# The additions to x and the moments of finished tiles, moved from the stage after an LSTM recurrence into the gaps of the recurrence itself

## What is computed

```python
def step(carry, x_t):
    h0, c0, h1, c1, a = carry
    xin = jnp.concatenate([x_t, a], axis=-1)
    h0, c0 = _lstm_cell(xin, h0, c0, Wi0, Wh0, bi0, bh0)
    h1, c1 = _lstm_cell(h0, h1, c1, Wi1, Wh1, bi1, bh1)
    q = h1 @ Wq.T
    attn = softmax(einsum('bh,bsh->bs', q, context))
    mixed = einsum('bs,bsh->bh', attn, context)
    a2 = jnp.tanh(jnp.concatenate([mixed, h1], axis=-1) @ Wo.T + bo)
    return ((h0, c0, h1, c1, a2), a2)

x = x + scan(step, layernorm(x))      # 1024 steps in time, batch of 4
x = x + ffn(layernorm(x))             # its input is quantized with max|layernorm(x)| over the whole tensor
...
```

## Time and profile before

| | |
|---|---|
| Time of the runs, median of 3 | 8434.98 us (8434.35 to 8435.3) |
| The profiled execution's own time | 8436.1 us |
| Its span, from first to last instruction | 8434.3 us |
| PE busy | 6828.4 us (81%) |
| PEld busy | 5803.5 us (69%) |
| DVE busy | 4235.9 us (50%) |
| ACT busy | 3225.4 us (38%) |
| POOL busy | 279.8 us (3%) |
| DMA | 62186 packets, 95.43 MB |
| Mean granted TensorE clock | 0.977 of 2.4 GHz |

### The profile page before, as it was taken

The page is one execution under the profiler, slowest core; times in us unless marked ns, Lnnn a source line. Parts: engine busy times, 40 slices in busy tenths (PEclk is TensorE's granted clock), DMA queues, the critical chain, the costliest instruction groups (busy, mean ns, idle before and its releaser), DMA issues. The chain is left out here.

```text
span 8434.3 us, 813385 instructions
## 1 busy us (share of the span) xinstructions
PE 6828.4 (81%) x380504; PEld 5803.5 (69%) x380505; DVE 4235.9 (50%) x21151; ACT 3225.4 (38%) x15030; POOL 279.8 (3%) x289
## 2 busy tenths in 40 slices
PE   6888888888888888888888888888888888776687
PEld 5777777777777777777777777777777777553454
DVE  5555555554554455455555455545545555565712
ACT  3333333333333333333333333333333333332322
POOL 0000000000000000000000000000000000012501
PEclk8999999999999999999999999999999999888798
DMA  2000000000000000000000000000000000000333
GB/s 85 5 0 0 0 0 0 0 0 0 0 0 0 0 0 0 0 0 0 0 0 0 0 0 0 0 0 0 0 0 0 0 0 0 0 6 18 111 116 112
DMA packets 62186, 95.43 MB, mean 11 GB/s; under 512 B 13633, under 2 KB 50497, under 8 KB 60993
## 3 DMA queue, kind: packets, MB, share of 16 engines
q1 hardware_dynamic: 59072, 86.54, 3.0%
q0 software_dynamic: 3072, 8.39, 0.3%
HBM read 74.99 MB, written 19.92 MB: 11 GB/s over the span
## 5 line engine op out<-in xcount | busy, mean ns | idle before, releaser
L304 PE MATMUL scan_sums<-rec_wh,scan_hT 128*4 128x64 f32 x131008 | 2392.1, 219 | 4.2 <-issue 4.1
L425 DVE STREAM_TRANSPOSE scan_sums<-scan_sums 128x64 f32<-128x64 f32 x6144 | 1546.0, 266 | 1137.6 <-PE scan_sums L304 1137.3
L304 PEld LDWEIGHTS scan_sums<-rec_wh,scan_hT 128*4 128x4 f32 x131008 | 1989.5, 89 | 4.9 <-issue 4.9
L304 PE MATMUL scan_sums<-rec_wa,scan_aT 128*4 128x64 f32 (+1 forms) x65536 | 1104.3, 219 | 382.0 <-ACT scan_aT L385 382.0
L304 PEld LDWEIGHTS scan_sums<-rec_wa,scan_aT 128*4 128x4 f32 (+1 forms) x65536 | 915.4, 88 | 570.9 <-ACT scan_aT L385 570.9
L304 PE MATMUL scan_sums<-rec_wx,scan_xT 128*4 128x64 f32 (+1 forms) x65536 | 1292.1, 219 | 7.7 <-issue 6.8
L304 PE MATMUL scan_sums<-rec_wi,scan_hT 128*4 128x64 f32 (+1 forms) x65536 | 1102.5, 219 | 168.8 <-DVE scan_hT L475 165.2
L304 PEld LDWEIGHTS scan_sums<-rec_wi,scan_hT 128*4 128x4 f32 (+1 forms) x65536 | 913.6, 88 | 357.6 <-DVE scan_hT L475 353.9
L304 PEld LDWEIGHTS scan_sums<-rec_wx,scan_xT 128*4 128x4 f32 (+1 forms) x65536 | 1024.2, 89 | 8.4 <-issue 7.4
L365 ACT ACTIVATE scan_sums<-rec_bias 128x192 f32<-128x192 f32 x2050 | 687.2, 335 | 475.1 <-DVE scan_hT L475 469.5
L370 ACT ACTIVATE scan_tanh_f<-scan_sums 128x8 f32<-128x8 f32 x2048 | 364.1, 178 | 1187.9 <-DVE scan_sums L425 1187.9
(11 more groups left out here) (247 smaller groups left out, 5750.5 us busy)
## 6 DMA issues: line engine op xcount, KB each, us to landing
experts_bias<-in_b SPq DMA_DIRECT2D x40, 640.0 KB, 3.8
moe_w<-in_w SPq DMA_DIRECT2D x16, 1024.0 KB, 12.3
slots_x<-route_zero SPq DMA_DIRECT2D x40, 128.0 KB, 1.7
experts_x<-slots_x SPq DMA_DIRECT2D x40, 128.0 KB, 2.1
slots_y<-experts_y SPq DMA_DIRECT2D x40, 128.0 KB, 1.7
w_xres<-in_x_steps SPq DMA_DIRECT2D x8, 512.0 KB, 11.3
w_xres<-in_x SPq DMA_DIRECT2D x4, 1024.0 KB, 11.7
out<-w_xres SPq DMA_DIRECT2D x8, 512.0 KB, 3.0
```

What stands on the lines that cost most here:

```text
L304: last = nc.tensor.matmul(sums[layer][BANK[g]][32 * j:32 * j + ROWS[g], 0:64], state[:, k, FIRST[g]:FIRST[g] + ROWS[g]], weight[:, k, j, 6 ...
L425: nc.vector.transpose(turned[l][g], sums[l][g][:, 0:64]).then_inc(gates_turned[l][g], 1)
```

## The change

It adds four programs to the recurrence, each working on group g - 1 (the 128 steps that are finished) while the steps of group g run, for g from 1 to 7:

1. GpSimd (L297 to L302) waits until `a_hist` holds the group and until the transposes of the group before are done, and copies the eight pieces (b, k) of 128x128 into `part`.
2. VectorE, in gaps 0 and 1 of the group's steps 0 to 3, transposes a piece in blocks of 32x32 into `stage` (`turn_part`, L496). The blocks are then right within, but not in the right places.
3. SP (L314 to L323) waits for the eight transposes, writes them with 32 transfers, each of 32 partitions x 4 x 32 values, into `a_rows` in DRAM, where the blocks land in order, waits for all, and reads the four tiles back into `mid` with one transfer.
4. VectorE adds the four tiles to x in gaps 0 and 1 of steps 7 and 8 (`fold`, L501), forms the statistics in those of steps 9 and 10 (`spread`, L505 and L506) and 11 and 12 (`gather_moments`, L510 and L511), and keeps the moments in step 13 (`keep_moments`, L515).

VectorE's loop over the steps becomes two: steps 28 to 127 as before, and then a loop over g in which 14 steps are written out and an inner loop runs the other 114. Nothing in TensorE's and ScalarE's recurrence changes.

The stage after the recurrence keeps the additions and moments of the last group's four tiles. TensorE turns them straight out of `a_hist` (L624), before the weights. ScalarE takes the square roots of 28 tiles in one instruction and later of 4 (`deviations`, L641), and it, not VectorE, normalizes all 32 tiles (`normalize`, L645), with the weight copies (L637) between them. VectorE forms the factors (L685, L687) and the largest values (L693). GpSimd's copies are gone from the stage.

```diff
 def scan(nc, ins, xT_all, a_hist, xres, ffn, w_out_scratch, a_rows, w):
...
         with nc.Block() as block:
+            @block.gpsimd
+            def _(pool):
+                nc.gpsimd.sem_inc(staged, 2 * B)
+                with pool.Fori(1, NB) as g:
+                    for b in range(B):
+                        for k in range(2):
+                            pool.wait_ge(a_kept, g * P)
+                            pool.wait_ge(staged, 2 * B * g)
+                            nc.gpsimd.tensor_copy(part[:, b, k, :], a_hist[:, bass.ds(g * P - P, P), k, b]).then_inc(part_done, 1)
+
             @block.sync
             def _(sp):
...
                 sp.wait_ge(ffn["w_out_kept"], 16)
+                for g in range(1, NB):
+                    sp.wait_ge(staged, 2 * B * g + 2 * B)
+                    for b in range(B):
+                        rows = a_rows[b, bass.ds(g * P - P, P), :].rearrange("(q r) (j k u) -> j r k q u", q=4, j=4, k=2)
+                        for j in range(4):
+                            for k in range(2):
+                                sp.dma_start(rows[j][:, k], stage[32 * j:32 * j + 32, b, k, :].rearrange("p (q u) -> p q u", q=4)).then_inc(rows_out, 16)
+                    sp.wait_ge(rows_out, ROWS_OUT * g + ROWS_OUT)
+                    sp.wait_ge(folded, B * g)
+                    sp.dma_start(mid[:], a_rows[:, bass.ds(g * P - P, P), :].rearrange("b p d -> p b d")).then_inc(mid_in, 16)
...
+                def turn_part(g, b, k):
+                    dve.wait_ge(part_done, 2 * B * g)
+                    dve.wait_ge(rows_out, ROWS_OUT * g)
+                    nc.vector.transpose(stage[:, b, k, :], part[:, b, k, :]).then_inc(staged, 1)
+
+                def fold(g, b):
+                    x = tile_of(xres, g - 1, b)
+                    dve.wait_ge(mid_in, 16 * g)
+                    nc.vector.tensor_tensor(x, mid[:, b, :], x, ALU.add).then_inc(folded, 1)
+
+                def spread(g, b):
+                    dve.wait_ge(folded, B * g + B)
+                    nc.vector.memset(held[:, 0:1], 0.0)
+                    nc.vector.bn_stats(stats[:, b, :], tile_of(xres, g - 1, b)).then_inc(spread_done, 1)
...
+                def late(g, at):
+                    def between(gap):
+                        if gap == 2:
+                            return
+                        if at < 4:
+                            turn_part(g, at, gap)
+                        elif 7 <= at < 9:
+                            fold(g, 2 * (at - 7) + gap)
+                        elif 9 <= at < 11:
+                            spread(g, 2 * (at - 9) + gap)
+                        elif 11 <= at < 13:
+                            gather_moments(g, 2 * (at - 11) + gap)
+                        elif at == 13 and gap == 0:
+                            keep_moments(g)
+                    return between
...
-                with dve.Fori((PLAIN + 3 * FC + 1) // U, T // U) as i:
+                with dve.Fori((PLAIN + 3 * FC + 1) // U, P // U) as i:
                     t = i * U
                     for s in range(U):
                         step(t, s)
+                dve.wait_ge(ffn["x_in"], 16 * (B + 1))
+                LATE = 14
+                with dve.Fori(1, NB) as g:
+                    for at in range(LATE):
+                        step(g * P, at, late(g, at))
+                    with dve.Fori(LATE // U, P // U) as i:
+                        t = g * P + i * U
+                        for s in range(U):
+                            step(t, s)
...
 def add_attention_and_normalize(nc, raw, a_hist, xres, xn, norm_max, w):
...
+                for b in range(B):
+                    for k in range(2):
+                        last = nc.tensor.transpose(turned[b][:, P * k:P * k + P], a_hist[:, P * LAST:P * NB, k, b], w["ident"][:])
+                    last.then_inc(turned_done, 1)
...
+                act.wait_ge(eps_done, 1)
+                deviations(0)
+                for f in range(2):
+                    keep_weight(f)
+                act.wait_ge(shift_done, 1)
+                for n in range(B * LAST):
+                    normalize(n)
+                    if n == 2 * B:
+                        act.wait_ge(moments_done, B)
+                        deviations(1)
+                    if n % B == B - 1 and 2 + n // B < FC:
+                        keep_weight(2 + n // B)
+                act.wait_ge(shift_done, 2)
+                for n in range(B * LAST, NT):
+                    normalize(n)
...
```

More of the change, by code:

```diff
@@ L284, in scan @@
         seeded = [m.sem(f"seeded{l}") for l in range(2)]
-        with nc.Block() as block:
+        part = m.sbuf("part", [P, B, 2, P])
+        stage = m.sbuf("stage", [P, B, 2, P])
+        mid = m.sbuf("mid", [P, B, D])
+        stats, moments = m.sbuf("stats", [P, B, 6]), m.sbuf("moments", [P, B, 2])
+        held = m.sbuf("held", [P, 2])
+        part_done, staged, rows_out, mid_in, folded, spread_done, moments_done, moments_kept = (m.sem(n) for n in (
+            "part_done", "staged", "rows_out", "mid_in", "folded", "spread_done", "moments_done", "moments_kept"))
+        with nc.Block() as block:
+            @block.gpsimd
[7 more added lines that the diff above has]
+                            nc.gpsimd.tensor_copy(part[:, b, k, :], a_hist[:, bass.ds(g * P - P, P), k, b]).then_inc(part_done, 1)
             @block.sync
@@ L529, in _ @@
             def _(pool):
[L530 to L536, removed]
                 pool.wait_ge(max_done, 1)
@@ L549, in _, with keep_weight @@
                     last.then_inc(weight_done, 1)
[L550 to L556, removed]
             @block.scalar
             def _(act):
-                for f in range(FC):
+                def keep_weight(f):
                     act.wait_ge(weight_done, f + 1)
@@ L563, in _, with deviations, normalize @@
                                          weight_turned[f % 2][:, 0:D].rearrange("p (c n) -> p c n", c=KC), ACT.Copy).then_inc(weight_kept, 1)
[L564 to L567, removed]
+                def deviations(part):
+                    nc.scalar.activation(std[:, parts[part], :], moments[:, parts[part], :, 1], ACT.Sqrt, bias=eps[:]).then_inc(std_done, 1)
+                def normalize(n):
+                    g, b = n // B, n % B
+                    nc.scalar.activation(xn[:, g, b, :], xres[:, g, b, :], ACT.Identity, bias=shift[:, g, b:b + 1],
+                                         scale=rstd[:, g, b:b + 1]).then_inc(xn_done, 1)
+                act.wait_ge(eps_done, 1)
[13 more added lines that the diff above has]
+                    normalize(n)
                 act.wait_ge(weight_kept, FC)
@@ new lines, in largest @@
+                def largest(n):
+                    g, b = n // B, n % B
+                    dve.wait_ge(xn_done, n + 1)
+                    nc.vector.tensor_reduce(row_max[:, g, b:b + 1], xn[:, g, b, :], AX.X, ALU.max,
+                                            apply_absolute_value=True).then_inc(row_max_done, 1)
+                add(0)
+                factors(0)
+                for b in range(1, B):
+                    add(b)
+                for b in range(B):
+                    spread(b)
@@ L599, in _ @@
+                for b in range(B):
+                    gather_moments(b)
+                for n in range(2 * B + 1):
+                    largest(n)
+                factors(1)
+                for n in range(2 * B + 1, NT):
+                    largest(n)
                 dve.wait_ge(row_max_done, NT)
```

73 lines of the change are left out of this document (44 added, 29 removed).

## The result

The changed kernel takes **8402.9 us** (median of 6 runs, 8400.25 to 8406.34); the kernel before took 8434.4 us beside it (6 runs, 8430.61 to 8435.3). The ratio is 0.9964, with a 95% interval of 0.9952 to 0.9976, which does not reach 1: 31.5 us, or 0.36%, faster. The forecast was 8402.7. The number is right, but two of the three terms it was made of are not: they erred in opposite directions.

A forecast was written before the change was run, and what follows sets the result against it. The bound was the recurrence's closed chain through TensorE, VectorE and ScalarE, 7.08 us a step, 1024 times, no engine full. Sum: 8435.0 - 50.5 (stage) + 9.8 (GpSimd wait) + 8.4 (jump back) = 8402.7 us; range 8388 to 8421.

The forecast's parts named there:

- The stage, -50.5 us: Stage after the recurrence: work leaves it, ScalarE's pitch of 0.43 us sets it; final reduction at 22.0 instead of 72.5 us.
- the upper price: Stage after the recurrence: ScalarE's pitch at 0.50 us instead of 0.43, making the stage 2.7 us longer.
- The wait for GpSimd, +9.8 us: Step 0 of a group: VectorE's first transpose waits for all eight GpSimd copies; 1.4 us late, seven times.
- Seven times: The wait for GpSimd's copies, 1.4 us, counted in all seven groups: 9.8 us.
- 1.4 us late: First transpose of a group: the recurrence goes on at 3.9 instead of 2.5 us, the whole chain waiting.
- The jump back, +8.4 us: VectorE's outer loop: code must be brought in by one transfer at each jump back, 1.4 us, six times.
- upper bound of 0 to 18: VectorE's outer jump: 0 if code is still there; 18 us if two transfers of 1.6 us follow each other.
- the rival "code is held": VectorE's outer loop: code is still held and the jump back costs nothing; 8394 us, chance 0.30.
- The transfers, 0: SP's 32 writes and read back take 21.4 us of 25.8 us of room, hidden by steps 4 to 6; no cost.
- the rival, 0.90 us: SP's transfers issue at 0.90 us and VectorE stands at the first addition; 8466 us, chance 0.07 (somewhat late, around 8432: 0.10).
- The gaps, 0: VectorE's idle gaps in the recurrence: added work of up to about 0.6 us each fits and costs nothing.
- This rival: Gaps too short: operations wait on each other or GpSimd slows VectorE; 1 to 3 us a group, 8410 to 8424 us, chance 0.11.

The follow-up runs named there:

- unrolled: Changed kernel with VectorE's seven groups written out one behind the other, no jump back over a group; 8386.7 us, ratio 0.9945.
- runs with 12 and 14 steps: Kernel before with only VectorE's new loop shape, 12 or 14 steps written out, nothing in the gaps, no transfers; 8454.5 and 8451.3 us.
- those with 4 to 10: Kernel before with only VectorE's new loop shape, 4, 8 or 10 steps written out; 8427.3, 8439.4 and 8424.4 us.
- early: Changed kernel with the additions in steps 5 and 6 instead of 7 and 8, all that follows two steps earlier; 8467.9 us.
- jump14: Kernel before with only VectorE's new loop shape, 14 steps written out, nothing in the gaps, no transfers; 8451.3 us.
- both: Changed kernel with VectorE's groups written out and each transpose waiting only for its own GpSimd copy; 8383.5 us, ratio 0.994.
- jump10: Kernel before with only VectorE's new loop shape, 10 steps written out, nothing in the gaps, no transfers; 8424.4 us.
- best: Changed kernel with groups written out, each transpose waiting for its own copy, and VectorE normalizing five of 32 tiles; 8383.3 us, ratio 0.9938.

## Why the prediction was right, and where it was not

**The stage, -50.5 us: right.** Measured -50.6. Its parts were less exact. ScalarE's normalizations follow each other at 0.485 to 0.52 us, not at 0.43, which was the upper price (+2.7 us); but ScalarE kept the first weights by 4.0 us after the last copy into the history instead of 4.9, and each of the later weight copies held up the normalization behind it by 0.26 us only (7358.51 to 7358.77). The errors cancel to 0.03 us.

**The wait for GpSimd, +9.8 us: wrong, measured +0.95.** The mechanism and the 1.4 us were right where nothing else stalls. Two steps of the working failed. "Seven times" added this wait to the one of the jump back, though both lie between the same two instructions of VectorE: GpSimd starts from the history's last copy whatever VectorE does meanwhile, and a stall of 3 us gives it all the time it needs. And "1.4 us late" took the wait's idle time for the delay of the step. Behind the transpose the sums of layer 1 were ready, so VectorE turned two of them back to back (983.37 us, 0.35 for both); `unrolled` measures 0.71 us of step for 1.34 of waiting.

**The jump back, +8.4 us: wrong size, measured +17.9, at the upper bound of 0 to 18.** That code is brought in and that this is paid six times was right, and so were the packets on the queue. The size was taken as one transfer's landing (1.4 us net). The idle time is 2.98 to 3.05 us. That is near the upper bound's two transfers of 1.6 us, but the bound's reason does not hold: only one packet lies within the stretch, the second starts after it. Some 1.1 us pass before that packet starts, and 1.5 us after its end; what fills them the trace does not show. On top of it comes the clock of TensorE, which the forecast left out: 2.8 of the 17.9 us.
The Trainium skill, "Runtime: NRT & Kernel Launch", section Instruction fetch mechanics, has the rule that decides here: a jump outside the held blocks forces a fetch. The runs with 12 and 14 steps agree (18 to 19 us), and those with 4 to 10 show the other side of it: there the rival "code is held" came true. Its size for what is held, two blocks of 256 instructions, the runs neither confirm nor refute: 315 instructions are fewer than 512, but a loop of that length can reach into three such blocks, and where the blocks begin no trace shows.

**The transfers, 0: right,** with 6 us to spare instead of 4.4. The pace of issue of the rival, 0.90 us, does not occur; 0.47 stands, and `early` shows what it costs when the room is gone.

**The gaps, 0: right.** All steps that hold an addition, a spread or a gather took 7.08 to 7.09 us like the others. (This rival was priced up to 8424 us, while the stated range ended at 8421.)

**Not foreseen, -0.8 us:** the recurrence's last two steps.

The sum: -50.6 + 0.95 + 17.9 - 0.8 = -32.6 us by the trace, with the start and the rest of the program (-2.4 and +2.2) -32.8 in the spans, and -31.5 in the medians. The forecast was -32.3. It came out because the term for the first of the two stalls was 8.9 us too large and that for the second 9.5 too small. That the first was too large is partly no accident, since the longer stall is what covers the shorter; that the two errors are of one size is luck.

## What to carry to other kernels

Before two stalls are added, see whether the second one's cause runs on during the first; if it does, only the longer one is paid, and once it is removed the other appears. A loop's body that is written out for a few special steps has a size at which its jump back begins to cost, in this program between 271 and 315 instructions of VectorE (elsewhere in a program it may be another) and 3 us of idle time a jump; if it is passed only a few times, write the passes out one behind the other, where the code comes in beside the work. Where a chain stalls, compare the steps and not the idle time of one engine: the chain can make up for half of a stall, or pay more, if TensorE's clock falls behind it.

## What the runs showed of the hardware

- **TensorE's clock after a short stall.** Idle times of 2.7 us in the midst of a recurrence that keeps TensorE busy at 2.4 GHz were followed by matmuls at 1.2 GHz in four of six cases of the changed kernel and three of six of `jump14`, for part of a step, at a price of 0.6 to 0.9 us. In `unrolled`, where VectorE stands for 1.4 us, the clock stayed at 1.00 in all seven groups.
- **Leaving a loop costs TensorE time too.** In the kernel before, its last two steps are written out behind its loop, and it idles there with nothing to wait for (timeline of PE in the kernel before, then TensorE's queue of instructions, q8, in 7310 to 7333 us):

```profile
7319.23 0.67 PE L304 MATMUL scan_sums<-rec_wh,scan_hT 128*4 128x64 f32 x33 [1.05 <-issue]
7322.96 0.22 PE L304 MATMUL scan_sums<-rec_wx,scan_xT 128*8 128x64 f32 x1 [1.76 <-issue]
7326.97 0.67 PE L304 MATMUL scan_sums<-rec_wh,scan_hT 128*8 128x64 f32 x33 [1.48 <-issue]
7330.69 0.22 PE L314 MATMUL scan_a_sum<-rec_woh,scan_hT 128*4 128x64 f32 x1 [0.52 <-issue]
```
```profile
q8 instruction: 5, 0.08, 1.5%
```

  Of these five packets of 16 KB the first four end 1.3 to 1.6 us before TensorE goes on from one of the four stalls. That they are what it waits for is read from this coincidence alone; no run changes TensorE's code. It costs 3.5 us in this run, 2.6 in the changed kernel and 4.6 in `both`; the amount differs from kernel to kernel, though this code is the same in all three.
- **The step itself is not quite constant.** From the first copy into the history to the one of step 1021 the runs without a stalled step differ by up to 8.5 us (before 7235.95, `jump10` 7228.46, `both` 7232.67, `best` 7236.93). That is 0.008 us a step, spread over all of them; its cause is open.
